# Value weights folded into the projection weights, and the low part of x made on the vector engine, in a convolution and attention kernel

## The reference, cut to what matters

```python
# layer 0: linear attention over raw and convolved q, k, v; 32 heads of 8 channels each per kind
qkv = concat(h @ wq.T, h @ wk.T, h @ wv.T)            # 768 channels
dw  = depthwise_5x5(qkv)                              # one 5x5 kernel a channel
pw  = grouped_1x1(dw)                                 # groups of 8 channels: 8x8 weights each
f   = concat(qkv, pw)
query, key_, value = relu(f_q), relu(f_k), f_v        # no relu on the value
scores = value_with_ones @ key_.T                     # per head, 9 x 8, over the 1024 pixels
out = scores @ query ; out = out[:8] / (out[8] + eps)
x1  = batchnorm(proj(out)) + x                        # 1x1 projection of 512 channels

# layer 1: softmax attention over 1024 x 1024 pixels
norm = (x1 - mean) / sqrt(var + eps)
attention = softmax(f(norm).T @ g(norm))
y = o(h(x1) @ attention.T) + x1
```

## Time and profile before

| what | value |
|---|---|
| median of 3 runs | 734.28 us (733.71 to 736.58) |
| the profiled execution: its time | 734.32 us |
| the profiled execution: its span | 732.5 us |
| PE busy | 666.1 us, 91% |
| DVE busy | 570.8 us, 78% |
| POOL busy | 530.7 us, 72% |
| ACT busy | 465.7 us, 64% |
| granted clock of PE, mean | 0.965 of full |

### The profile page before, as it was taken

The page is one execution under the profiler, slowest core; times in us unless marked ns, Lnnn a source line. Parts: engine busy times, 40 slices in busy tenths (PEclk is TensorE's granted clock), DMA queues, the critical chain, the costliest instruction groups (busy, mean ns, idle before and its releaser), DMA issues.

```text
span 732.5 us, 8826 instructions
## 1 busy us (share of the span) xinstructions
PE 666.1 (91%) x3276; PEld 494.2 (67%) x3276; DVE 570.8 (78%) x669; ACT 465.7 (64%) x735; POOL 530.7 (72%) x248
## 2 busy tenths in 40 slices
PE   4979998999999999989989999899899956997998
PEld 3844456765777788655767887658687842475887
DVE  6999626998889999979889999888899992342231
ACT  3764443898867678797767867977686571232231
POOL 3449993989998999899989998899989782000000
PEclk9999997999999999999999999999999996899999
DMA  7000001000110000001100000000100000000000
GB/s 284 1 0 1 0 0 58 1 1 0 59 58 0 30 16 16 1 0 58 44 15 15 16 30 0 1 1 1 58 15 15 30 0 0 1 1 0 15 15 29
DMA packets 4938, 16.25 MB, mean 22 GB/s; under 512 B 800, under 2 KB 928, under 8 KB 3872
## 3 DMA queue, kind: packets, MB, share of 16 engines
q1 hardware_dynamic: 4896, 15.69, 5.8%
HBM read 11.50 MB, written 4.19 MB: 21 GB/s over the span
## 4 chain that ended last, share of the span: by engine, by line
PE 58%; ACT 16%; DVE 14%; POOL 7%; issue 3%; DMA 1%; SPq 0%; POOLq 0%; DVEq 0%; ACTq 0%
PE ps L585 12%; PE ps L561 11%; PE ps L495 8%; ACT prod L841 7%; POOL rows L1268 7%; DVE ps L1063 6%; PE ps L662 5%; PE ps L596 3%; PE ps L576 3%; DVE small L1200 2%; PE ps L448 2%; ACT kt L855 2%; PE ps L710 2%; PE ps L504 2%; ACT vt L856 2%
## 5 line engine op out<-in xcount | busy, mean ns | idle before, releaser
L1268 POOL TENSOR_TENSOR conv<-conv,prod 128x930 f32<-128x930 f32 (+4 forms) x192 | 422.6, 2232 | 40.8 <-ACT prod L841 37.3
L1063 DVE SCALAR_TENSOR_TENSOR ps<-raw,dw_sb,ps 128x960 f32<-128x960 f32 (+4 forms) x290 | 348.3, 1201 | 7.6
L841 ACT ACTIVATE prod<-raw,dw_sb 128x930 f32<-128x930 f32 (+4 forms) x228 | 247.3, 1138 | 35.1 <-POOL conv L1268 22.4
L585 PE MATMUL ps<-ht,pt 128*128 128x256 f32 x512 | 115.1, 379 | 0.0
L585 PEld LDWEIGHTS ps<-ht,pt 128*128 128x128 f32 x512 | 95.1, 190 | 11.8
L1268 POOL TENSOR_TENSOR rows<-rows,prod 128x930 f32<-128x930 f32 (+4 forms) x36 | 82.9, 2304 | 22.0 <-ACT prod L841 17.2
L984 ACT ACTIVATE rows<-ps,small 128x1024 f32<-128x1024 f32 x32 | 35.6, 1113 | 76.9 <-DVE small L1204 76.9
L1200 DVE TENSOR_REDUCE small<-ps 128x1 f32<-128x1024 f32 x32 | 39.1, 1221 | 33.0 <-PE ps L561 33.0
L561 PE MATMUL ps<-hi,t_hi 128*128 128x512 f32 x128 | 46.9, 449 | 13.1 <-ACT rows L984 13.1
L448 PE MATMUL ps<-hi,wqkv_hi 128*128 128x512 f32 x96 | 40.6, 423 | 11.3 <-DVE lo L350 10.2
L855 ACT ACTIVATE kt<-ps 128x256 f32<-128x256 f32 x68 | 31.7, 469 | 29.8 <-PE ps L618 26.5
(11 more groups left out here) (134 smaller groups left out, 1080.2 us busy)
## 6 DMA issues: line engine op xcount, KB each, us to landing
q_raw<-x_dram SPq DMA_DIRECT2D x4, 1024.0 KB, 6.4
x<-x_dram SPq DMA_DIRECT2D x4, 1024.0 KB, 4.8
out_dram<-x_t SPq DMA_DIRECT2D x16, 256.0 KB, 2.3
conv<-wqkv_dram SPq DMA_DIRECT2D x1, 768.0 KB, 4.5
conv<-fg_dram SPq DMA_DIRECT2D x1, 512.0 KB, 5.8
proj_sb<-proj_dram SPq DMA_DIRECT2D x1, 512.0 KB, 7.6
pw_sb<-pw_dram SPq DMA_DIRECT2D x1, 384.0 KB, 6.8
mask_sb<-masks_dram SPq DMA_DIRECT2D x1, 264.0 KB, 6.2
```

The costliest lines, as they stand in the source:

```text
L585: mm = pe.matmul(dst[:, 0:C], pt[:, i % PT_BUFS, j, :], ht[:, j, :], start=(j == 0), stop=(j == NB - 1))
L841: act.activation(dst, view, ACT.Copy, scale=weight(t, i)).then_inc(prod_ready, 1)
L1063: return dve.scalar_tensor_tensor(dst, view, w, before, ALU.mult, ALU.add)
L1268: pool.tensor_tensor(total, total, product, ALU.add).then_inc(conv_pool, 1)
```

## The change

Three things. (1) The value tiles of the convolution are only transposed (a product with the identity, `pe.transpose`) and no longer multiplied by their pointwise weights; instead two products at the start multiply these weights, stored transposed, with the convolved half of the projection weights, and ACT copies the result over `proj_sb`. (2) `lo` of images 2 and 3 is made by DVE at the end of its `body(0)` and `body(1)`, no longer by POOL. (3) `CARRY` falls from 16 to 12, and several tables that place DVE taps and ACT products move entries by one or a few.

```diff
-CARRY = 16
+CARRY = 12
-TAPS_SCORES_PW, TAPS_DEN_PW, TAPS_SCORES_RAW, TAPS_DEN_RAW = 8, 3, 1, 0
-TAPS_Q_PW = (2, 4)
+TAPS_SCORES_PW, TAPS_DEN_PW, TAPS_SCORES_RAW, TAPS_DEN_RAW = 8, 3, 2, 0
+TAPS_Q_PW = (2, 3)
-TAPS_FOLD = (0, 1)
+TAPS_FOLD = (1, 1)
-TAPS_MAX = (2, 3, 2, 1, 3, 2, 3, 4, 2, 4)
+TAPS_MAX = (2, 3, 2, 1, 3, 2, 3, 4, 2, 2)
-LATES_PWKV = (2, 1, 0, 1, 0, 1, 0, 1)
-LATES_RAWKV = (2, 0, 2, 2, 6, 5, 11, 5)
+LATES_PWKV = (3, 1, 0, 1, 0, 1, 1, 0)
+LATES_RAWKV = (5, 0, 3, 1, 5, 4, 14, 3)
-PRODUCTS_MB = 3
-PRODUCTS_X1 = (3, 0, 2, 1)
-PRODUCTS_X1T = (1, 0, 0, 1)
-PRODUCTS_FOLD = 4
+PRODUCTS_MB = 5
+PRODUCTS_X1 = (3, 1, 1, 1)
+PRODUCTS_X1T = (0, 0, 0, 0)
+PRODUCTS_FOLD = 5
-PRODUCTS_EXP = (3, 2, 3, 1, 0, 4, 3, 6, 11, 4)
-PRODUCTS_ATT = (0, 3, 2, 1, 1, 5, 4, 8, 1, 7)
+PRODUCTS_EXP = (3, 2, 3, 1, 0, 4, 4, 6, 14, 5)
+PRODUCTS_ATT = (0, 3, 2, 1, 0, 4, 4, 8, 1, 10)
...
                     for t in range(CK, TILES):
-                        c0 = (t - CK) * P
-                        mm = pe.matmul(dst[:, c0:c0 + P], conv[:, t, j * P:(j + 1) * P], pw_sb[:, t, :],
-                                       start=True, stop=True)
+                        c0, block = (t - CK) * P, conv[:, t, j * P:(j + 1) * P]
+                        if t < 2 * CK:
+                            pe.matmul(dst[:, c0:c0 + P], block, pw_sb[:, t, :], start=True, stop=True)
+                        else:
+                            mm = pe.transpose(dst[:, c0:c0 + P], block, ident)
...
             mm.then_inc(vec_full, 1)
+            pe.wait_ge(fg_ready, 1)
+            for h in range(CK):
+                mm = pe.matmul(ps[:, 5, h * C:(h + 1) * C], pw_sb[:, 2 * CK + h, :], proj_sb[:, CK + h, :],
+                               start=True, stop=True)
+            mm.then_inc(value_weights_full, 1)
...
             pe.wait_ge(vec_ready, 1)
+            pe.wait_ge(value_weights_ready, 1)
...
             act.copy(fg[:], ps[:, 5, :].rearrange("p (k m) -> p k m", k=CK)).then_inc(fg_ready, 1)
+            act.wait_ge(value_weights_full, 1)
+            act.copy(proj_sb[:, CK:2 * CK, :], ps[:, 5, :].rearrange("p (k m) -> p k m", k=CK)).then_inc(
+                value_weights_ready, 1)
...
                 taps(DVE_TAPS)
+                if b + 2 < B:
+                    split_lo(dve, b + 2)
...
                 if b + 1 < B:
                     conv_adds(b + 1, RSTD_AT[1], POOL_ADDS)
-                if b + 2 < B:
-                    split_lo(pool, b + 2)
...
+    pw_bd[:, 2 * CK:] = pw_bd[:, 2 * CK:].transpose(2, 1, 0).copy()
```

More of the change, by code:

```diff
@@ L244, in conv_seq_kernel @@
         vec_ready = sem("vec_ready")
+        value_weights_full = sem("value_weights_full")
+        value_weights_ready = sem("value_weights_ready")
         hi_ready = sem("hi_ready")
```

## The result

The kernel with the change took 740.41 us (median of 8 runs, 736.40 to 741.51), the kernel before beside it 732.97 (8 runs): a ratio of 1.0083, 95% interval 1.0061 to 1.0106. The same two kernels in a later session gave 1.0093 (1.0067 to 1.0119). The forecast was 743.2 us, 8.9 more than the median it started from; measured are 7.4 us more by the medians of the two kernels side by side, and 7.3 in the later session. A ratio is worked out over all runs and can differ a little from the quotient of the two medians. The profiled execution after took 738.87 us with a span of 737.1, at a mean granted clock of 0.967.

What follows compares the result with a forecast made beforehand. POOL's late adds were taken to bound the first 26 us of a body, PE the rest. Start 1.0, ACT's order 0.7, `lo` 5.6, fold 1.8, less 0.2, made 8.9 on 734.3: 743.2 us; own range 741 to 745.5, 8-in-10 range 731 to 747.

Steps and rivals of the forecast that it cites:

- the rival in which `lo` is cheap: `lo` on DVE slips between POOL's adds or is not held up by them: 739.8 us; chance 0.14.
- Late adds are not helped by taking `lo` from POOL: Start of a body: POOL's nine late adds wait for ACT's product, so removing `lo` does not start them earlier.
- Transposes: Value blocks on PE: 0.12 us saved each, 7.6 us in four bodies, but ahead of L636, where POOL sets the end.
- The start: Two weight products and ACT's copy delay ACT's first drain from 31.29 to about 32.3: +1.0 us, from 0.6 to 1.5.
- ACT's late order: Raw unit 1 drained after all 10 late products, L636 at T + 26.9: +1.1 us; +0.7 taken in body 0.
- `lo` on DVE: Start of bodies 1 and 2: halves at 3.04 us beside POOL's adds, L636 at T + 28.6: +2.8 each, +5.6 us.
- The fold: A tap placed between the fold and `fold_lo` delays `fold_lo`: +0.6 us in bodies 0 to 2, +1.8 us.
- Body 3: First block full 0.24 us earlier, so ACT's first late product and POOL's first add are too: -0.2 us.
- The product tables: Other table entries put ACT's products one or two places earlier; POOL waits some 3 us less a body; taken as 0.
- PE as the bound: Rival: late adds do not hold L636 and PE's 7.6 us come through, less 1.0 at the start: 727.7 us; chance 0.16.
- The clock: Rival: PE's new wait before L636 brings one more clock fall in bodies 1 and 2 each: 746.6 us; chance 0.09.
- Transposes that slow it: Rival: transposes do not count as work, PE's clock falls in each body's first blocks: 750.0 us; chance 0.02.

Runs made afterwards that it cites:

- after_lo_in_gap: Changed kernel with `lo` on DVE moved ahead of the last three taps and two `x_t`: 737.93 us against 734.48 for the kernel before, 1.0046.
- lo_only: Kernel before with `lo` at the end of DVE's body, none on POOL, tables and `CARRY` 16 kept: 734.73 us against 734.69, 1.0005.
- value_only: Kernel before with only the value transposes and the weights product at the start; constants and `lo` as before: 737.19 us against 734.69, 1.0017.
- tables_only: Kernel before with all constants of the change, `CARRY` 12 included, no value weights, `lo` on POOL: 735.68 us against 734.69, 1.0020.
- after_lo_on_pool: Changed kernel with `lo` put back on POOL: 738.01 us against 734.69 for the kernel before, 1.0058.
- after_early_lates: Changed kernel with two late ACT products ahead of its first drains and `lo` on DVE ahead of its last taps: 727.90 us against 734.11, 0.9921.

## Why the prediction was right, and where its sizes were off

The direction and the mechanism came out. The closeness of the number is in part luck, and the number alone does not prove the mechanism: 740.4 us lies just below the forecast's own range of 741 to 745.5 and nearer to the 739.8 of the rival in which `lo` is cheap. What decides between the two is the trace, with halves of 2.32 and 3.20 us, and after_lo_in_gap, where the same halves take 2.35 together and Q is 0.8 us earlier.

**Late adds are not helped by taking `lo` from POOL: shown.** They start at T + 3.6 in bodies 2 and 3 alike, with POOL idle for 6.66 us. In lo_only alone the 4.69 us of `lo` became 4.76 us of idle time.

**Transposes: as predicted**, 0.25 us a block for the 0.24 worked out. The list of groups:

```profile
L621 PE MATMUL ps<-pw_sb,conv 128*128 128x128 f32 x128 | 22.7, 305 | 7.9 <-ACT vt L866 7.9
...
L623 PE MATMUL ps<-mask_sb,conv 128*128 128x128 f32 x64 | 13.2, 291 | 0.0
```

The last part of the prediction put 128 + 64 instructions on the line of products. It is 128: half of the 256, the other half being 64 value products of two instructions, which are the 64 of L623 now. The saving is waited away, but not where I had it: at ACT's drains of the first blocks (2.2 us, and 0.6 ahead of L450), and only 0.4 at the bank of unit 5. value_only shows such waits without the rest of the change.

**The start: +1.0 predicted, +1.5 at the first drain.** ACT and PE there, beside the earlier trace rows:

```profile
32.30 0.58 ACT L1035 COPY proj_sb<-ps 128x512 f32<-128x512 f32 x1 [3.85 <-PE ps L779]
32.78 0.39 ACT L865 ACTIVATE kt<-ps 128x256 f32<-128x256 f32 x1
```

```profile
25.93 1.89 PE L753 MATMUL ps<-conv 128*128 128x256 f32 x8
...
31.15 1.11 PE L779 MATMUL ps<-proj_sb,pw_sb 128*128 128x256 f32 x4
```

L753 does what stood at 25.41 before, ahead of anything the change adds, so 0.5 of the 1.5 is not the change's, and 1.0 is. The other traces bear this out: from PE's first product of the start's h and o weights (23.68 before, 24.20 after) to ACT's first drain of a block it is 7.61 to 7.62 us in the four kernels with the old start and 8.57 to 8.58 in seven of the ten with the new one (more in the other three). At the start of body 0 it can't be read off: in single traces that start lies between 120.4 and 122.3 us with the old start and between 121.0 and 124.4 with the new one. So of the 1.8 us in the table 1.0 is shown to be the change's at the first drain, and the rest was not traced.

**ACT's late order: +1.1 predicted, +1.0 shown** by tables_only, +0.8 by after_lo_on_pool. In body 0 it was +0.25, inside the 0 to 1.1.

**`lo` on DVE: right in kind, too dear by 1.1 us a body.** This is the term that was mis-sized. Predicted: 3.04 us a half, a joining tap of 3.27, DVE's last tap at T + 27.7, Q at T + 28.6, +2.8 in each of two bodies. Measured in body 2: 2.32 + 3.20 us, a joining tap of 2.93, last tap at T + 26.5, Q at T + 27.5, +1.7. The error was to take one mean price for a cost that depends on the phase within POOL's add. The prediction had the rule (DVE waits for the running add to end) and did not use it for the price. Its own cheap example shows the phase too: the tap at 104.83 did not run alone, an add of POOL had 0.23 us left, and the tap ended 1.09 us after it. Half by half in body 2: the first met an add that had run for 0.9 of its 2.1 us. That is 0.55 us less for the pair, 0.35 for the tap and 0.15 for a start at T + 4.45; together 1.05 a body, 2.1 of the 8.9. POOL's usual add beside it was 2.1 to 2.3 us, not the 2.4 of the prediction, and the late adds ended at T + 27.1, not T + 26.8.

**The fold: +0.6 predicted, +0.4 measured**, 1.2 and not 1.8 us in three bodies. `fold_lo` started at 511.59, when the tap that began at 510.40 was done. **Body 3: -0.2 predicted, -0.4** in length, -0.2 of it at L640 (T + 25.35 for T + 25.57). **The product tables: nothing predicted.** POOL's wait for products fell from 7.6 to 4.4 us without a gain for PE.

Anew: 1.8 + 0.25 + 2 x 1.7 + 1.2 - 0.4 = 6.25 us. From the 734.3 that the forecast started from this gives 740.5, but that it meets the 740.4 so well is chance: the kernel before took 732.97 beside it, and of the 7.4 us between the two 1.1 to 1.2 are not in the sum. The forecast of 8.9 was 2.65 too high in these terms (`lo` 2.2, the fold 0.6, ACT's order in body 0 0.45, body 3 0.2, less 0.8 at the start). The part without an account stands against that, so the forecast missed the measured difference by 1.5 us and not by 2.65.

**The rivals.** PE as the bound did not happen: its 7.6 us are in waits. `lo` cheap: true wherever no add runs (lo_only, after_lo_in_gap, after_early_lates), not where the change puts it. The clock: the stretches moved, but not as I had priced them; in bodies 0 to 2 of the profiled execution two went and two came. Transposes that slow it: in body 2 the two transposes of every block take 0.38 us and the granted clock is 1.00, but in body 1 the last two blocks ran at half clock:

```profile
287.37 0.63 PE L623 MATMUL ps<-mask_sb,conv 128*128 128x128 f32 x2
```

They stand behind new waits for ACT's drains, nothing was lost by it at Q, and value_only, with the same transposes, has a clock of 1.00 over its whole body 1. So transposes alone do not bring the fall; whether the waits do was not tested.

## What to carry to other kernels

Ask of work taken from an engine what that engine waits for next; here the released 4.7 us became idle time, and two products moved into ACT's idle time ahead of its first drain made the kernel before 6.2 us faster, 2.5 of them seen at L636. Where two chains meet at one instruction, undoing one alone moves that instruction only as far as the other lets it; undo both before saying what each costs, and look at the instruction as well as at the time. An instruction of DVE that reads two SBUF tensors should be placed where POOL waits, and priced by the phase of POOL's running add, not by a mean.

## What the runs showed of the hardware

DVE instructions with two SBUF inputs of 128x1024 took 1.22 us (`lo`) and 1.29 us (the tap) with no add in the way, and 1.25 to 3.27 us beside one, ending 1.08 to 1.11 us after the add that was running, 80 times out of 80. POOL's add behind the pairs shown above took 2.98 to 3.08 us instead of 2.1 to 2.3. The Trainium skill, GPSIMD Engine Reference, Specifications, names the shared SBUF interfaces and this kind of instruction; the traces agree and add the price, at most one whole add of POOL.

The clock falls are not fixed to a place: 4.53 us for the second energy block before and 2.95 after, with the same instructions and the same 1.53 us wait ahead of them. I had priced a new wait as bringing another fall; the new wait before L636 brought none in body 2, whose granted clock is 1.00. What moved the falls was not found.
